# Moving the input loads ahead of the stores in SyncE's order, and GpSimd's differences ahead of its masks in the first steps

## What is computed

```python
p2 = x[:, :, _I2] * x[:, :, _J2]
y2 = jnp.einsum('bgihw,goi->bgohw', p2, W2).reshape(B, Ch, H, Wd) + b2[None, :, None, None]
p3 = x[:, :, _I3] * x[:, :, _J3] * x[:, :, _K3]
y3 = jnp.einsum('bgihw,goi->bgohw', p3, W3).reshape(B, Ch, H, Wd) + b3[None, :, None, None]
return inp + y2 * beta2 + y3 * beta3 * CONV3_SCALE
```

```python
theta = l[:, :c_red]
f = jnp.einsum('niab,nicd->nabcd', theta, theta)
f = jax.nn.softmax(f.reshape(n, h * w, h, w), axis=1)
f = jax.nn.softmax(f.reshape(n, h * w, h * w), axis=2)
out = jnp.einsum('nabcd,nicd->niab', f, g)
```

## Time and profile before

| | before |
|---|---|
| time, median of 3 runs | 5301.48 us (5292.23 to 5304.6) |
| time of the profiled execution | 5297.93 us |
| span of the profiled execution | 5296.1 us |
| PE busy | 5202.1 us, 98% |
| ACT busy | 5093.0 us, 96% |
| POOL busy | 4423.2 us, 84% |
| DVE busy | 4411.7 us, 83% |
| last `TH` DMA of layer 0 issued | 796.3 us |

### The profile page before, as it was taken

One profiled execution on the slowest core, in us unless ns is written; L12 is line 12 of the kernel. 1 busy time (PEld: TensorE's weight loads), 2 busy tenths in 40 slices (PEclk: granted clock), 3 DMA queues, 4 the chain that ended last, 5 costly groups with the idle time before them and its releaser, 6 DMA issues.

```text
span 5296.1 us, 88127 instructions
## 1 busy us (share of the span) xinstructions
PE 5202.1 (98%) x32182; PEld 2521.4 (48%) x32182; DVE 4411.7 (83%) x8859; ACT 5093.0 (96%) x2948; POOL 4423.2 (84%) x1854
## 2 busy tenths in 40 slices
PE   8989999999999999999999999999999999999999
PEld 3333335444545454444554454544454545444454
DVE  7878888888888888888888888888888888888887
ACT  7878779999999999999999999999999999999998
POOL 6656555788888998899899888899888899889988
PEclk9999999999999999999999999999999999999999
DMA  6777762222223222222222222222222322222222
GB/s 135 159 156 166 148 134 59 43 62 63 62 62 63 62 62 61 57 52 52 56 62 60 58 60 62 50 57 62 62 63 62 62 62 62 61 58 53 50 41 49
DMA packets 227275, 380.45 MB, mean 72 GB/s; under 512 B 158181, under 2 KB 175262, under 8 KB 216734
## 3 DMA queue, kind: packets, MB, share of 16 engines
q1 hardware_dynamic: 225728, 373.82, 33.9%
q10 hardware_dynamic: 1118, 1.00, 0.1%
HBM read 259.08 MB, written 102.74 MB: 68 GB/s over the span
## 4 chain that ended last, share of the span: by engine, by line
PE 64%; ACT 17%; issue 8%; DVE 3%; POOL 3%; SPq 3%; DMA 2%; DVEq 0%; POOLq 0%
PE at_AV L1284 30%; PE at_S L1243 17%; ACT at_ring L1027 12%; PE at_AV L1290 9%; ACT at_ring L1033 5%; PE l_TY L607 3%; SPq L457 2%; PE at_AV L1280 2%; PE l_SEL L596 1%; PE l_TY L614 1%; DVE at_ring L1100 1%; DMA l_TH<-l_YO 1%; DVE l_U L564 1%; POOL l_LO L500 1%; POOL l_XX L491 1%
## 5 line engine op out<-in xcount | busy, mean ns | idle before, releaser
L1100 DVE TENSOR_SCALAR_CACHE_REDUCE at_ring<-at_S 128x1344 f32<-128x1344 f32 (+2 forms) x2352 | 2882.0, 1242 | 456.8 <-PE at_S L1243 438.5
L977 POOL TENSOR_TENSOR at_ZP<-at_ZP,at_ring 128x1568 f32<-128x1568 f32 x640 | 2263.5, 3571 | 146.8 <-ACT at_ring L1033 136.7
L1284 PE MATMUL at_AV<-at_ring,at_GT 128*64 128x392 f32 x12800 | 2299.0, 500 | 6.8 <-issue 5.9
L1027 ACT ACTIVATE at_ring<-at_ring,at_NM 128x3136 f32<-128x3136 f32 x784 | 2274.1, 2901 | 12.0 <-DVE at_NM L1109 10.8
L1033 ACT ACTIVATE at_ring<-at_ring,at_RZ 128x3136 f32<-128x3136 f32 x784 | 2275.3, 2902 | 0.0
L1284 PEld LDWEIGHTS at_AV<-at_ring,at_GT 128*64 128x64 f32 x12800 | 854.3, 137 | 1145.3 <-issue 1108.9
L1243 PE MATMUL at_S<-at_THM,at_THS 128*128 128x448 f32 x5376 | 1380.4, 386 | 11.6 <-DVE at_ring L1100 9.2
L1243 PEld LDWEIGHTS at_S<-at_THM,at_THS 128*128 128x128 f32 x5376 | 926.1, 188 | 631.7 <-DVE at_ring L1100 289.9
L998 POOL TENSOR_TENSOR at_OUTB<-at_OUTB,at_ZB 128x1568 f32<-128x1568 f32 x246 | 877.3, 3566 | 16.8
L1290 PE MATMUL at_AV<-at_ring,at_ones 128*32 128x392 f32 x7168 | 677.0, 498 | 2.9 <-DVE at_ACC L1193 2.9
L564 DVE TENSOR_TENSOR l_U<-l_TY,l_XB 128x512 f32<-128x512 f32 x784 | 487.1, 683 | 150.4 <-PE l_TY L607 150.2
(11 more groups left out here) (86 smaller groups left out, 2481.8 us busy)
## 6 DMA issues: line engine op xcount, KB each, us to landing
at_THM<-hld SPq DMA_DIRECT2D x128, 392.0 KB, 6.5
at_THS<-hld SPq DMA_DIRECT2D x256, 192.0 KB, 4.1
l_X<-in_x SPq DMA_DIRECT2D x124, 392.0 KB, 7.5
at_CIN<-att SPq DMA_DIRECT2D x62, 406.0 KB, 7.6
at_ZB<-rzd SPq DMA_DIRECT2D x62, 406.0 KB, 7.6
yd<-l_YO SPq DMA_DIRECT2D x128, 196.0 KB, 5.4
att<-at_ACC SPq DMA_DIRECT2D x248, 98.0 KB
at_OUTB<-yd SPq DMA_DIRECT2D x62, 392.0 KB, 8.6
```

Source lines behind the costliest of these rows:

```text
L977: e.tensor_tensor(z, z, v, ALU.add).then_inc(g_add, 1)
L1027: e.activation(v, v, ACT.Exp, bias=NM[:, i:i + 1], accum_out=ZS[:, i:i + 1]).then_inc(a_p1, 1)
L1100: e.tensor_scalar(ring[:, s % RING, SC * a_:SC * b].rearrange("p (b w) -> p b w", w=SC), PS[:, k % 2, bank:bank + b - a_, 0:SC], 1.0, None ...
L1284: ins = e.matmul(dst[64 * j:64 * j + 64, 0:QC], GT[fl.n % 2][:, keys_of(fl.n, t), :], ring[:, slot, q:q + QC], start=(i == 0), stop=(i == ...
```

## The change

In `sync`, the loads of image `n + 3` are issued at the head of the loop's body, ahead of the wait for the close of image `n`, and so ahead of its `TH` copies and its stores, where they had stood behind both. With them goes their wait for POOL's differences of image `n`. In `gpsimd`, the differences of steps 1 and 2 stand ahead of the mask of the next step, as those of step 0 did.

```diff
         for n in range(n_img):
+            if n + NX < n_img:
+                load(n + NX)
             e.wait_ge(v_t, y_use(last_step(n)) + 1)
             if n >= 1:
                 e.wait_ge(g_h, 2 * n)
...
             for m in range(4):
                 e.dma_start(yd[n, 16 * m:16 * m + 16], YO[n % 2][32 * m:32 * m + 16, :]).then_inc(s_st[n % 2], 16)
-            if n + NX < n_img:
-                load(n + NX)
             if n >= 1:
                 split_out(n - 1)
...
         for u in range(NU):
-            if u == 0:
-                parts(0)
+            if u < 3:
+                parts(u)
             if u + 1 < NU:
                 masked(u + 1)
-            if u:
+            if u >= 3:
                 parts(u)
```

## The result

The changed kernel is slower: 5317.96 us in the median of 6 runs (5314.02 to 5321.25) against 5298.8 us (5292.23 to 5305.33, 6 runs), a ratio of 1.0035 with a 95% interval of 1.0022 to 1.0048. That is 19 us more, where I had forecast 5300, about no change, and a range up to 5314.

A forecast was written before the change was run, and what follows sets the result against it. Layer 0 was taken as bound by a ring of close, eight `TH` issues, landing, split, difference and PE. 5297.9 − 0.9 + 0 + 0 = 5297.0, against the median 5300.6, given as 5300 us; range 5287 to 5314.

The forecast's parts named there:

- The ring: Layer 0: close, eight issues, landing, split, difference, PE, close; 24.03 us for one image, counting some 30 times.
- The gain of the loads: POOL's waits for loads, 40 to 780 us: gain 0 from moving the loads, bound 27.7 us.
- The differences: Steps 1 and 2 at the start: PE's selection of step 2 earlier, 0.9 us gained, bounds 0.3 and 1.9.
- SyncE's time: SyncE's issues ahead of the `TH` copies: moved loads fit the same gap, cost 0, bound 1 us behind image 16.
- Then the queue: DMA queue ahead of the `TH` copies: loads land before the last copy, cost 0, bound 3 us together.
- ordinary image: Images without layer 1 transfers: loads land about 119, last `TH` copy issued about 121.2, margin 2.2 us, cost 0.
- seven others: Images followed by layer 1 transfers: 1 to 4 us of issue off the margin, 0.5 us each, 3 together.
- What may scatter: Slow clock and slow `TH` issues in layer 0, dealt anew without known cause: from −14 to about +14 us.
- The range: Whole run, 5287 to 5314 us: bounds of the unknown costs, with the runs' own spread of 12 us inside.
- the bounds of +3, +1 and +14: +3 us for early transfers, +1 for SyncE's time behind image 16, +14 for slow clock and slow issues.
- the signs that I had set down as wrong: Profile signs: `TH` landing above 3 us often, `TH` issues after close, ring shorter 1 us, layer 1 over 3 us off.
- Rival 2: Last of eight `TH` copies waits behind loads landing above 9.7 us after issue: 5329 us, 0.5% slower; chance 0.07.

The follow-up runs named there:

- Kernels 6: The kernel before with `SPLIT_LATE` = 7 instead of 5, so POOL makes the key parts two steps later: 5234.68 us, ratio 0.9880.
- kernel 9: The kernel before with the first of each image's eight `TH` copies split into halves, so nine issues: 5322.82 us, ratio 1.0050.
- kernel 5: The kernel before with the loads issued right behind the `TH` copies and ahead of the stores: 5297.49 us, ratio 0.9999.
- kernel 1: The kernel before with only the differences of steps 1 and 2 moved, loads in their old place: 5296.72 us, ratio 0.9997.
- 3: The changed kernel with the loads issued last in the same image's iteration, behind key stores and early transfers: 5311.88 us, ratio 1.0027 against the kernel before.
- Kernel 2: The kernel before with only the loads moved to the head of the loop, differences in their old place: 5316.55 us, ratio 1.0034.
- kernel 4: The changed kernel with loads from image 3 on fetching half the columns, same issues and order: 5298.44 us, ratio 1.0004 against the kernel before.

## Why the prediction was wrong

**The ring was right.** I had said that close, issues, landing, split, difference and PE set each image of layer 0, and that what lengthens that counts once per image. Kernels 6 and 9 show it from both sides.

**The gain of the loads was right at 0.** Their waits fell from 27.7 us to none, and kernel 5 shows that this alone is worth nothing.

**The differences were right.** 0.9 us forecast, 0.7 measured at the first `TH` copy in kernel 1, and not to be seen in the time. In the changed kernel itself that copy is only 0.3 us earlier (42.63, where I had said 42.0), and PE's selection of step 2 starts at 16.27, not 15.6; single starts scatter by some 0.6 us between kernels.

**SyncE's time was right.** The key stores took over the slow issues (4.29 and 1.82 us behind image 2), and the four loads then went out in 1.82. Even behind image 16 they were issued by 466.89, 1.7 us ahead of the next `TH` copy at 468.55.

**"Then the queue" is the step that failed**, in its ordinary image and in its seven others. For the seven I charged the early transfers with their issue time, 1 to 4 us, and allowed 0.5 us of delay each, 3 us together. They also have bytes: behind images 8 and 10 two of 392 KB, behind 12 and 14 four of 192 KB, some 0.8 MB each time, which at the 211 GB/s of the earlier trace rows is 3.7 us in the same queue ahead of the loads. Behind image 16 they are only eight of 8 KB, and there the 0.5 us contradict my own terms: 3.55 us of issues out of a margin of 2.2 leave the last copy 1.4 us late, and it was 2.0 (3.58 against 1.60). Landing grew by 5.5 us in sum, not 3 at most, and all of it right behind such transfers. For the ordinary image the arithmetic held (loads over before the eighth issue), but I compared only with the last copy. The loads were in flight in the 2 us about the close, and the issues there took 2.9 us more, a term that I had not put in the sum. It is no draw: the three kernels with the whole loads right ahead of the copies (after, 2 and 3) have 163.5 to 165.2 us of issues, the other four with eight issues and `SPLIT_LATE` = 5 have 159.8 to 161.7. The instruction packets are the likely cause.

**"What may scatter" was the second failure.** I took the slow clock and the slow issues for a draw that falls to either side. They have a direction. In the seven kernels with `SPLIT_LATE` = 5 and eight issues (217 rounds), the time from the close to the rounding is over 6.8 us in 89, and 44 of these are followed by slow clock ahead of the next close; of the 128 shorter ones, 1 is. Each stretch costs 1.4 to 1.7 us. This makes +6.7 of the 14.8 us of layer 0, the largest part, and the three kernels with the whole loads right ahead of the copies have 8, 11 and 9 stretches against 3, 4, 5 and 5 in the other four. But the length of that one way doesn't decide it: of the 22 rounds of kernel 9 with 7.16 to 7.39 us, only 1 has slow clock, and in the seven kernels 9 of the 25 between 7.1 and 7.4. What else decides is open.

**The range did not add up its own terms.** On 5300.6, the bounds of +3, +1 and +14 give 5318.6, and I wrote 5314. The measured 5317.96 lies under that sum, but that would have been luck: the +14 stood for a draw, and the slow clock and the slow issues were no draw. Of the signs that I had set down as wrong, layer 1 starting over 3 us off came true (14.8 us at the last image's first `TH` issue); single `TH` copies landed more than 3 us after their issue in 12 images instead of 7.

**Rival 2 named the right place and sign with the wrong bar.** I had it decide when loads land more than 9.7 us after their issue. The median landing after is 7.1 us (line L422):

```profile
DMA to landing us min/median/max: 4.1/7.1/16.1
```

Once the start is over, the bar was passed only behind images 8, 10, 12 and 14 (10.8 to 12.0 us); behind image 16, where the copies landed latest, the loads landed in at most 8.8 us, but had been issued late. The 19 us came from three smaller effects. The Trainium skill's rule ("DMA: Bandwidth & Descriptors", section "Queues, rings and completion order"), that each DMA engine takes an issuing engine's descriptors in ring order, is what the packets show: behind image 8, 12544-byte packets for 4 us and the waiting 3136-byte ones after them. I had set it aside because the median landing left 2.2 us of margin.

**What stays open.** That the instruction packet makes the `TH` issue slow is argued from their coincidence (24 of 25 in the two kernels, and 137 of the 145 `TH` issues of over 0.76 us in all twelve traces begin within 0.7 us of such a packet's start), not tried: no kernel moved the packets alone. Nor was it tried what delays them; kernel 4, with half the bytes in flight, lacks the changed kernel's slow issues in images 3, 5, 13, 14 and 15, which fits the loads. The sums come from one execution each; that the median's 19 us divide as the 16 of the profiled execution do is assumed. Kernel 2 shows how far one can lie off: its profiled execution has 11 us more from H to the next S than the changed kernel's, while its median is 1.4 us lower.

## What to carry to other kernels

A transfer that is off the path can be moved at no gain and still cost, if it is moved right ahead of a small one that an engine waits for: sum the bytes in flight at that moment, together with the issue times that push them back, and don't compare with a median landing. Where each round of a loop waits for a small transfer, the better change is to put more work of the waiting engine ahead of the wait: here one constant gave 1.2%, where the order of the loads could only lose 0.35%. And a pause of TensorE can cost more than its length when slow clock follows the longer ones more often, so such stretches don't belong in a symmetric scatter.

## What the runs showed of the hardware

Slow clock (0.50 granted, 1.2 GHz) came in 44 of 89 rounds with over 6.8 us from the close to the rounding and in 1 of 128 with less, but in only 6 of the 31 rounds of kernel 9, all of which have over 6.8. A 16 KB packet on the instruction queue goes with a DMA issue of 0.8 to 1.8 us instead of 0.59 in the kernels before and after. Behind image 2 the four loads are issued in 4.14 us behind the stores of 196 KB each (before) and in 1.82 us behind the key stores of 98 KB each (after), and the first four key stores take 2.65 us behind the loads and 4.29 behind the stores: an issue's length goes with what was issued ahead of it.
